# Turning every second head's probabilities by a DMA transpose instead of by TensorE and a copy

## The reference

```python
x = x + attn(_layernorm(x))                 # per token: 16 x 16 scores between its heads, RoPE on q and k
x = x + xattn(_layernorm(x), ctx_2048)      # 2048 queries against 2048 keys
x = x + moe(_layernorm(x))                  # 8 experts, the best 2, and a shared one

# xattn: what the change touches
q = _fq_sym(q * scale, axis=-1)             # rounded to 127 steps of its largest element
k = _fq_sym(k, axis=-1)
v = _fq_sym(v, axis=2)
attn = einsum('bhqd,bhkd->bhqk', q, k)      # 16 heads x 2048 x 2048
attn = softmax(attn, axis=-1)
attn = _fq_unsigned(attn, axis=-1)          # rounded to 255 steps of the row's largest
out  = einsum('bhqk,bhkd->bhqd', attn, v)
```

## Time and profile before

| | |
|---|---|
| median of 3 runs | 1080.78 us (1079.26 to 1083.98) |
| profiled execution | span 1079.2 us from its first to its last instruction; the profile gives no other time for it |
| busy | PE 82%, DVE 88%, ACT 84%, POOL 79% of the span |
| granted TensorE clock | mean 0.978 of 2.4 GHz |

### The profile page before, as it was taken

The page is one execution under the profiler, slowest core; times in us unless marked ns, Lnnn a source line. Parts: engine busy times, 40 slices in busy tenths (PEclk is TensorE's granted clock), DMA queues, the critical chain, the costliest instruction groups (busy, mean ns, idle before and its releaser), DMA issues.

```text
span 1079.2 us, 30117 instructions
## 1 busy us (share of the span) xinstructions
PE 890.3 (82%) x11283; PEld 619.1 (57%) x11424; DVE 944.3 (88%) x1818; ACT 905.9 (84%) x1083; POOL 857.3 (79%) x874
## 2 busy tenths in 40 slices
PE   6966868888888888888888888888888888888886
PEld 4533545656566656565656565566566666556554
DVE  4987878998989898999989898999999898988883
ACT  2534979989999999989989999989899899989892
POOL 7668978898888989898989989898988889842020
PEclk9976989999999999999999999999999999999998
DMA  6011000000000000000000000000000000000000
GB/s 224 1 40 44 4 4 2 7 6 7 6 7 7 6 2 12 2 7 7 7 7 7 7 2 12 1 7 7 6 7 7 7 7 2 2 6 2 7 2 11
DMA packets 8438, 14.00 MB, mean 13 GB/s; under 512 B 1635, under 2 KB 6246, under 8 KB 7910
## 3 DMA queue, kind: packets, MB, share of 16 engines
q1 hardware_dynamic: 8294, 12.06, 3.3%
HBM read 9.96 MB, written 2.10 MB: 11 GB/s over the span
## 4 chain that ended last, share of the span: by engine, by line
PE 57%; ACT 19%; issue 12%; DVE 10%; POOL 1%; DMA 0%; POOLq 0%; SPq 0%; ACTq 0%; DVEq 0%
PE ps_score L1478 15%; PE ps_score L1489 14%; ACT prob_t L822 11%; PE ps L1343 10%; ACT prob L810 7%; DVE score L1123 6%; PE ps_pv L1505 4%; PE ps L1552 3%; PE ps_score L1343 2%; PE ps L1582 1%; PE ps L1528 1%; PE ps L1459 1%; DVE hs L1059 1%; POOL hs L436 1%; PE ps L1464 1%
## 5 line engine op out<-in xcount | busy, mean ns | idle before, releaser
L1123 DVE TENSOR_SCALAR_CACHE_REDUCE score<-ps_score,q_neg 128x1024 f32<-128x1024 f32 x512 | 645.4, 1281 | 73.8 <-PE ps_score L1478 67.9
L810 ACT ACTIVATE prob<-score,exp_bias 128x2048 uint16<-128x2048 f32 x256 | 513.9, 2008 | 12.5 <-DVE exp_bias L1133 12.5
L1478 PE MATMUL ps_score<-keys,queries 128*128 128x512 bf16 x883 | 276.9, 383 | 127.9 <-ACT prob_t L822 76.8
L822 ACT COPY prob_t<-ps_score 128x1024 int32<-128x1024 int32 x240 | 242.5, 1011 | 68.6 <-PE ps_score L1489 65.3
L1489 PE MATMUL ps_score<-ident_f,prob 128*128 128x128 f16 x4096 | 272.9, 220 | 29.3 <-issue 23.8
L1489 PEld LDWEIGHTS ps_score<-ident_f,prob 128*128 128x128 f16 x4096 | 240.3, 98 | 91.8 <-issue 76.5
L1478 PEld LDWEIGHTS ps_score<-keys,queries 128*128 128x128 bf16 x1024 | 69.2, 97 | 211.8 <-issue 153.8
L552 POOL TENSOR_TENSOR folded<-product 128x512 f32<-128x512 f32 x128 | 160.2, 1275 | 4.8 <-DVE ho L1082 3.1
L542 POOL TENSOR_TENSOR product<-hs_exp,v_tok 128x1024 f32<-128x1024 f32 x64 | 149.5, 2349 | 1.6 <-ACT hs_exp L778 1.6
L542 POOL TENSOR_TENSOR product<-qk_rot 128x1024 f32<-128x1024 f32 x64 | 149.5, 2351 | 0.2 <-POOL qk_rot L535 0.2
L560 POOL TENSOR_TENSOR folded<-folded 128x256 f32<-128x256 f32 x128 | 92.8, 749 | 0.0
(11 more groups left out here) (142 smaller groups left out, 1227.2 us busy)
## 6 DMA issues: line engine op xcount, KB each, us to landing
prob_t<-in_w SPq DMA_DIRECT2D x3, 1024.0 KB, 5.1
x_in<-in_x SPq DMA_DIRECT2D x16, 128.0 KB, 2.1
score<-in_cond_t SPq DMA_DIRECT2D x4, 512.0 KB, 6.9
out<-x_out SPq DMA_DIRECT2D x16, 128.0 KB, 1.7
w_qkv<-in_w_qkv SPq DMA_DIRECT2D x1, 768.0 KB, 4.3
early<-in_w_kv SPq DMA_DIRECT2D x1, 512.0 KB
w_s<-in_w_s SPq DMA_DIRECT2D x3, 128.0 KB
w_o<-in_w_o SPq DMA_DIRECT2D x1, 256.0 KB
```

The costliest lines, as they stand in the source:

```text
L810: act.activation(prob[:, s, :].bitcast(U16), score[:, s, :], ACT.Exp, bias=exp_bias[:, s:s + 1], scale=-1.0, accum_out=prob_sum[:, t.par, ...
L822: act.copy(prob_t[:, t.count(H, h) % KEPT].rearrange("p k q -> p (k q)").bitcast(I32), ps_score[:, slot(h + TURN, 2)].rearrange("p b k -> ...
L1123: dve.tensor_scalar(score[:, s, HALF * i:HALF * i + HALF], ps_score[:, slot(h, i)].rearrange("p b k -> p (b k)"), q_neg[:, t.par, h:h + 1] ...
L1478: mm = pe.matmul(ps_score[:, slot(h, i), b, :], queries[:, t.par, h // 2, h % 2, :], keys[:, h // 2, k0:k0 + KEYS], start=True, stop=True)
```

## The change

The odd heads' probabilities no longer pass through TensorE, a slot and a copy. SP issues a DMA transpose from `prob` to `prob_t`, which counts up one of six semaphores `prob_turned`. The even heads are turned by TensorE as before and are all copied by ScalarE; VectorE copies none. The slots are given out in the order of use (`PLACE`), so that their alternation closes over the missing turns, and the values' product waits for both kinds.

```diff
-DVE_KEEPS = (13,)
+BY_DMA = tuple(range(1, H, 2))
...
+def by_dma(n):
+    return n % H in BY_DMA
...
+def score_uses():
+
+    uses = []
+    for n in range(T * H + TURN):
+        if n < T * H:
+            uses += [("score", n, 0), ("score", n, 1)]
+        if n >= TURN and not by_dma(n - TURN):
+            uses.append(("turn", n - TURN, 0))
+    return uses
+
+
+USES = score_uses()
+PLACE = {u: i for i, u in enumerate(USES)}
...
-        def slot(h, i):
-
-            return (h + i) % 2
+        def score_slot(n, i):
+
+            return PLACE["score", n, i] % 2
...
+            def turn(h, t):
+
+                n = t.count(H, h)
+                sp.wait_ge(prob_ready, n + 1)
+                sp.sem_inc(settled, 1)
...
+                if (due := t.due(H, h - KEPT + 1)) is not None:
+                    sp.wait_ge(pv_done, due)
+                    sp.sem_inc(settled, 1)
+                sp.dma_start_transpose(prob_t[:, n % KEPT], prob[:, h % RING, :]).then_inc(prob_turned[n % KEPT], 16)
+
             def body(t):
                 for h in range(H):
+                    if t.exists() and by_dma(h):
+                        turn(h, t)
...
-                if (due := t.due(H, h - RING + 1)) is not None:
-                    act.wait_ge(turn_made, due)
+                if (before := t.due(H, h - RING + 1)) is not None:
+                    if by_dma(before - 1):
+                        act.wait_ge(prob_turned[(before - 1) % KEPT], 16 * count_dma(before, (before - 1) % KEPT))
+                    else:
+                        act.wait_ge(turn_made, count_pe(before))
...
-                    if h >= TURN and t.exists() and h not in DVE_KEEPS:
+                    if h >= TURN and t.exists() and not by_dma(h - TURN):
                         keep_turned(h - TURN, t)
...
+            def wait_slot(u):
+
+                if u >= 2:
+                    kind, n, i = USES[u - 2]
+                    if kind == "score":
+                        pe.wait_ge(score_kept, 2 * n + i + 1)
+                    else:
+                        pe.wait_ge(turn_kept, count_pe(n + 1))
+
...
-                pe.wait_ge(turn_kept, t.count(H, h + G))
+                for n in range(t.count(H, h), t.count(H, h + G)):
+                    if by_dma(n):
+                        pe.wait_ge(prob_turned[n % KEPT], 16 * count_dma(n + 1, n % KEPT))
+                if (made := count_pe(t.count(H, h + G))) > 0:
+                    pe.wait_ge(turn_kept, made)
```

More of the change, by code:

```diff
@@ L99, in pairs, with count_dma, count_pe @@
         return self.idx // 2 * n + extra
+def by_dma(n):
+    return n % H in BY_DMA
+def count_dma(n, s):
+    return sum(by_dma(i) and i % KEPT == s for i in range(n))
+def count_pe(n):
+    return sum(not by_dma(i) for i in range(n))
+def score_uses():
[8 more added lines that the diff above has]
+PLACE = {u: i for i, u in enumerate(USES)}
 def over_tiles(body):
@@ L285, in layer_kernel @@
         turn_kept = sem("turn_kept")
+        prob_turned = [sem(f"prob_turned{i}") for i in range(KEPT)]
         pv_done = sem("pv_done")
@@ L881, in body @@
                         head_exp(n)
-                    if h >= TURN and t.exists() and h not in DVE_KEEPS:
+                    if h >= TURN and t.exists() and not by_dma(h - TURN):
                         keep_turned(h - TURN, t)
-                    if h < TURN and m.exists() and h not in DVE_KEEPS:
+                    if h < TURN and m.exists() and not by_dma(h - TURN):
                         keep_turned(H + h - TURN, m)
@@ L1122, in keep_scores @@
                             dve.wait_ge(q_chain, t.count(5, 5))
-                    dve.tensor_scalar(score[:, s, HALF * i:HALF * i + HALF], ps_score[:, slot(h, i)].rearrange("p b k -> p (b k)"),
+                    dve.tensor_scalar(score[:, s, HALF * i:HALF * i + HALF], ps_score[:, score_slot(t.count(H, h), i)].rearrange("p b k -> p (b k)"),
                                       q_neg[:, t.par, h:h + 1], None, ALU.mult, ALU.min,
@@ L1134, in bias @@
                                   ).then_inc(bias_ready, 1)
[L1136 to L1142, removed]
             def cross_sum(t):
@@ L1470, in scores @@
                     pe.wait_ge(q_kept, t.count(2, 2))
[L1472 to L1475, removed]
+                n = t.count(H, h)
+                wait_slot(PLACE["score", n, i])
                 for b in range(2):
                     k0 = HALF * i + KEYS * b
-                    mm = pe.matmul(ps_score[:, slot(h, i), b, :], queries[:, t.par, h // 2, h % 2, :],
+                    mm = pe.matmul(ps_score[:, score_slot(n, i), b, :], queries[:, t.par, h // 2, h % 2, :],
                                    keys[:, h // 2, k0:k0 + KEYS], start=True, stop=True)
@@ L1482, in turn @@
             def turn(h, t):
[L1483 to L1487, removed]
+                n = t.count(H, h)
+                pe.wait_ge(prob_ready, n + 1)
+                wait_slot(PLACE["turn", n, 0])
+                out = ps_score[:, turn_slot(n)].rearrange("p b k -> p (b k)").bitcast(F16)
                 for i in range(T):
@@ L1647, in body @@
                         ho_project(n)
-                    if h >= TURN and t.exists():
+                    if h >= TURN and t.exists() and not by_dma(h - TURN):
                         turn(h - TURN, t)
-                    if h < TURN and m.exists():
+                    if h < TURN and m.exists() and not by_dma(h - TURN):
                         turn(H + h - TURN, m)
```

16 lines of the change are left out of this document (10 added, 6 removed).

## The result

The changed kernel takes 1072.81 us (median of 7 runs, 1065.04 to 1077.59), the kernel before 1079.69 us beside it (1079.11 to 1083.98). The ratio is 0.9932, with a 95% interval of 0.9905 to 0.9959. The sign is the forecast's, the time lies inside the range of 1036 to 1256 us but above the likeliest case's own 1036 to 1068, and the gain of 6.9 us is under a quarter of the forecast one. The seven runs of the changed kernel have spans of 1063.2 us (mean granted clock 0.945) to 1075.8 us (0.93), and the ones between them lie at 0.932 to 0.939; the profiled execution is the longest, 1077.59 us with span 1075.8, so its trace shows somewhat more of the loss than the median has. The kernel before has 0.978.

A forecast was written before the change was run, and what follows sets the result against it. A loop across four nearly full engines, not one bound: 26 us off the steady stretch, 2 ahead, 5 behind, 4.4 added at the end, -29, so 1052 us (likeliest case, 0.50, own range 1036 to 1068); range 1036 to 1256.

The forecast's parts named there:

- The transposes are hidden: Between a head's probabilities and its values' product: landing in 6.9 us, bracket 3.4 to 10.5, costs zero except at the end.
- The packet bound: DMA transpose cut into 2048 packets of 256 bytes at 69 ns: 8.8 us of service, 10.5 to landing; kernel 1254 us.
- late transposes: Rival, 0.14: landings past 6.1 us stall TensorE's in-order queue at the values' product; at 10.5 us, about 1150 us.
- their rate: Rival, 0.10: a transpose needing over 7.5 us of service sets the pace; at 8.8 us the kernel takes 1254 us.
- blocks one after another: Rival, 0.10: a head's sixteen 128 x 128 blocks transfer in turn, 1.7 us each, 27 us a head; about 3600 us.
- The relief: Busy time per tile falls: VectorE 54.8 to 53.5 us, ScalarE 54.4 to 47.3, TensorE 50.8 to 42.4.
- GpSimd is late next: GpSimd, unchanged, sets the next floor at 57.4 us a tile; tile taken as 57.6, from 59.65.
- I take 74% as safe, at no cost.: TensorE busy 42.4 of a 57.6 us tile, 74%, was taken to keep its granted clock, at no cost.
- VectorE's wait for scores: In the steady stretch, VectorE's wait for score products was to halve from 3.5 to 1.75 us a tile.
- The clock was a rival: Rival, 0.03: at 1.2 GHz score products' 0.59 us doubles, costing 4.8 us a tile against 2.95 gained; about 1105 us.
- The sum: Whole kernel: -26 in the stretch, -2 ahead, -5 behind, +4.4 at the end, -29 us; span 1079.2 to 1050.
- The tail: Last tile's head 15: nothing hides its transpose, so its values' product starts 4.4 us later.

The follow-up runs named there:

- norm-first kernel: The changed kernel with GpSimd's norm of x_one put ahead of the two score products before it: 1058.31 us, 0.9802.
- the wait filled: The changed kernel with 36 unread products on TensorE just ahead of its wait for the normed x_one: 1056.54 us, 0.9781.
- the norms on ScalarE: The changed kernel with GpSimd's norm of x_one first and two of GpSimd's three norms given to ScalarE: 1053.91 us, 0.9769.
- the late norm: The kernel before, without DMA transposes, with GpSimd's norm of x_one moved behind the choice of experts: 1193.32 us, 1.1060.
- the fastest versions: Changed kernel, x_one's norm first, two norms on ScalarE, very last head turned by TensorE: 1049.37 us; the same with 18 unread products ahead of x_one's turn: 1047.10 us.

## Why the prediction was right in sign and wrong in size

**The transposes are hidden: right.** They land in 4.3 us, inside the bracket of 3.4 to 10.5, under the 6.9 taken and under the 6.1 us of the tightest group. The packet bound failed in its price: (274534 - 8294) / 128 = 2080 packets each, near the 2048 thought, but (0.388 x 1075.8 - 0.033 x 1079.2) x 16 us over 266240 packets is 23 ns a packet, not 69. That is 3.0 us of all 16 engines for 512 KB. The Trainium skill's 350 to 400 GB/s (Advanced Engine Details and Errata, X-Bar Transpose (TRN2)), an estimated 1.3 to 1.5 us, is half of this, but its point, that the transfer is quick, holds. The Trainium skill's 1309 ns for one 128 x 128 by DMA (VectorE: DVE Perf Modes, The three transpose paths) can't be carried over to a head as the rival did: sixteen such blocks land in 4.3 us together, not in the estimated 20.9 us. The page gives the time of one block; that sixteen follow one after another was the prediction's reading, not its rule. The rivals of late transposes, of their rate and of blocks one after another fall with this.

**The relief: right, with one row short.** With the clock held (the tile from 700.37 us) ScalarE is busy 47.8 us (47.3 forecast) and VectorE 53.4 (53.5). TensorE has 44.0, not 42.4. Missing records are the likely reason: the trace of before has 706 score products, 219.5 us, in the stretch for the 824 that 206 heads need, and the norm-first kernel, with all 844 of its own, shows 250.5 us for them, 0.297 each, so that (824 x 0.297 - 219.5) / 12.875, about 2 us a tile, were missing from my sum. TensorE was fuller than I read, before and after.

**GpSimd is late next: right, and I stopped there.** The chain goes through it, its full-clock tile is 58.1 us against the floor of 57.4, and with two norms taken from it the one tile at full clock lasts 57.1. But I asked only what pace it sets, not who waits for it in order. TensorE does, at the norm's turn.

**The step that failed: "I take 74% as safe, at no cost."** The clock does not follow the mean share of a tile: that is 44.0 / 58.1 = 76% in the tile at 1.00 and 78% in the one at 0.92. TensorE stands 2.8 us (at most 3.3) at one place in it, and behind that the granted clock goes to 0.50 (500 to 505 us). A clock below 1.00 in the stretch was one of the prediction's own signs of being wrong. Filling that idle time with unread work returned 16.3 of the 20.8 us by which the changed kernel missed the forecast; making the norm early returned 14.5, both together 15.5, and so they are one loss. It is the clock and not the wait: the tile from 700.37 us has the wait too, keeps its clock and lasts 58.1 us, as a tile without the wait does.

```profile
738.25 0.44 PE L1391 MATMUL ps<-ident,normed 128*128 128x128 f32 x2 [2.70 <-POOL normed L482]
...
855.65 0.44 PE L1391 MATMUL ps<-ident,normed 128*128 128x128 f32 x2 [2.70 <-POOL normed L482]
```

Behind the first of these the clock stays at 1.00, behind the second it falls (the tile from 817.51 us has 0.93 and lasts 60.3 us). So the length of the wait alone doesn't decide it, and what does is open. The Trainium skill, TensorE: Matmul & The Clock Gate, section HAM oscillation, describes such a loop, in which a wait in each pass, there for a DMA, sends the engine back to half rate; the windows at 495 to 515 us agree, but here the loop falls back in eight of twelve tiles and not in each. The clock was a rival at 0.03, as a fall to 1.2 GHz for the whole kernel; what happened is a fall for some 10 us in each of five tiles, worth 61.5 - 58.1 = 3.4 us, a shorter one in three, worth 2.2 to 2.5, and little in the other four.

**VectorE's wait for scores: wrong.** It should have halved from 3.5 us a tile. With the clock held it is 46.5 us (the wait filled) and 52.3 us (the norm first), 3.5 and 4.0 a tile. The new row is TensorE's wait at a turn for VectorE's drain, 1.07 us each, 52 times with the wait filled. It comes at the same four of a tile's eight turns each time: 0.6 us at `h` = 4, 0.8 at 6, 1.05 at 14, and 1.8 at `h` = 0 of the next tile, where head 14 is turned. TensorE stands there in order, with the next head's scores behind the turn. By `PLACE` a turn always takes the slot of its own block's first score half. In the block before no head is turned, so that the second half now waits for VectorE alone and goes out earlier, and the turn then has to wait for the drain of the first half; before, the wait for ScalarE's copy came ahead of that second half and covered it. This fits the rows, but no run changed the order of the slots, so it is argued and not shown. At `h` = 0 VectorE has two short operations of the experts (L1235, L1238), 1.3 us together, between the two drains, and this wait is the longest:

```profile
678.12 0.69 DVE L1235 SCALAR_TENSOR_TENSOR early<-early,ps 128x512 f32<-128x512 f32 x1
...
680.88 1.46 PE L1539 MATMUL ps_score<-ident_f,prob 128*128 128x128 f16 x16 [1.78 <-DVE score L1178]
```

These are of the filled version; the clock falls there as well, in this tile and three others of its trace.

**The sum.** In the filled version the exponentials go from 97.2 to 1022.7 us, 27.2 us less than the earlier trace rows, where I had 33; ahead of them it is 1.3 less; behind them 32.6 us stand for 28.0. That is -23.9 from a span of 1079.2, against -28.6. The tile is 58.1 to 58.5 us, not 57.6. The wait for scores, which stayed at 3.5 us a tile where 1.75 were forecast, is the likely place of the rest; no run took it away.

**The tail: the sum was right, its parts were not.** It grew by 4.6 us (4.4 forecast).

```profile
1045.12 0.19 ACT L865 ACTIVATION_READ_ACCUMULATOR prob<-score,exp_bias 128x1 f32 x1
...
1049.89 1.24 PE L1558 MATMUL ps_pv<-prob_t,values 128*32 128x128 f16 x64 [1.99 <-issue]
```

From the probabilities to the product it is 4.6 us, 2.1 more than the 2.5 before; the other 2.5 come behind it, where the clock is lower: 0.78 from 1045 to 1055 us, against 0.99 in the kernel before from 1053 to 1063. With the norms on ScalarE, turning the last head by TensorE gave back 4.5 us and most of the clock (0.89 for 0.73).

## What to carry to other kernels

When work is taken off an engine that runs in order, find the place in the loop where it will now stand still for an engine that was not relieved, and price that place by its idle time and by what a lost clock behind it would cost, not by the mean busy share. Then bring the late producer's short operation ahead of its long ones: here it was worth nothing before the change and 14.5 us after it. What has no work behind it to hide a transfer, as the last head, is better left where it was.

## What the runs showed of the hardware

- Idle times of 2.6 to 3.3 us in the changed kernel were followed by a granted clock of 0.50 in eight of twelve tiles, and by none in four, where they lasted 2.7 us; the 4.7 to 5.0 us of the late norm, by a fall in each tile. Such a fall lasted up to some 10 us (the windows at 495 to 515 and at 608 to 632 us), though TensorE was over 90% busy in it. 18 unread products in the gap were as good as 36 within the intervals.
- A DMA transpose of 128 x 2048 fp16 between two buffers of SBUF lands in 4.3 us, in 4.5 us when one starts every 3.7 us. SP needs a median of 1.9 us to issue one. At a DMA share of 0.37 the kernel was 0.12% slower (0.03 to 0.21%) and no engine's instructions were longer, but the small transfers beside it were: x's load from 2.1 to 3.1 us, the output's store from 1.7 to 2.6.
- The clock of the fastest versions still means 0.96 to 0.97 in the stretch. Its falls come behind waits as short as 1.4 us (the third norm, followed by another of 0.95 us) and 1.8 us (the turn of head 14). Whether filling these, or another order of the slots, would bring anything is open; neither was tried.
